# Two local-attention blocks and a gated sum in one phase

## What is computed

```python
for d in range(2):                        # two local blocks
    half = shift(x[:, C//2:], by=1)       # upper channels come from the token before
    q, k, v = split(concat(x[:, :C//2], half) @ wqkv[d])      # 8 heads of 64
    q = l2norm(q) * q_scale[d]; k = l2norm(k) * k_scale[d]
    q, k = rotate(q, k)                   # rotary angles with a scale by position
    a = softmax(q @ k.T + window_mask)    # 64-token windows, each sees itself and the one before
    x = x + (a @ v) @ wo[d]
    y = layernorm(concat(x[:, :C//2], shift(x[:, C//2:], by=1))) * ln_g[d] + ln_b[d]
    u, g = split(y @ w1[d] + b1[d])       # 341 hidden channels each
    x = x + (u * gelu(g)) @ w2[d] + b2[d]
out = x_row + silu(x) * s                 # s: output of the state-space part before it
```

## Time and profile before

| | us |
|---|---|
| median of 3 runs (4225.66 to 4240.99) | 4240.4 |
| the profiled execution | 4256.1 |
| its span, first to last instruction | 4253.9 |
| PE busy in the span | 3659.6 (86%) |
| DVE, ACT, POOL busy | 2656.3, 2155.1, 861.8 |
| mean granted clock of TensorE | 0.919 of 2.4 GHz |

### The profile page before, as it was taken

One profiled execution on the slowest core, in us unless ns is written; L12 is line 12 of the kernel. 1 busy time (PEld: TensorE's weight loads), 2 busy tenths in 40 slices (PEclk: granted clock), 3 DMA queues, 4 the chain that ended last, 5 costly groups with the idle time before them and its releaser, 6 DMA issues. The chain is left out here.

```text
span 4253.9 us, 74287 instructions
## 1 busy us (share of the span) xinstructions
PE 3659.6 (86%) x27416; PEld 2097.3 (49%) x27416; DVE 2656.3 (62%) x5977; ACT 2155.1 (51%) x4957; POOL 861.8 (20%) x1067
## 2 busy tenths in 40 slices
PE   5988878888989996899899899988878887887887
PEld 3655654444545543333333333445555665555555
DVE  5667646565555654776766767736655665665665
ACT  3555554554555453565555655754554554444454
POOL 1111000000010002122232132124212331431421
PEclk8999988988999898899999999989998998999999
DMA  3222301111101102111011111002120230321112
GB/s 107 62 48 45 77 20 47 36 24 31 36 17 43 29 13 91 28 32 38 17 43 32 23 37 33 15 38 62 37 71 23 61 80 8 79 61 27 53 42 54
DMA packets 146011, 183.15 MB, mean 43 GB/s; under 512 B 29972, under 2 KB 99796, under 8 KB 142324
## 3 DMA queue, kind: packets, MB, share of 16 engines
q1 hardware_dynamic: 139748, 170.93, 16.0%
q10 hardware_dynamic: 5904, 7.48, 0.7%
HBM read 91.69 MB, written 34.08 MB: 30 GB/s over the span
## 5 line engine op out<-in xcount | busy, mean ns | idle before, releaser
L1266 ACT ACTIVATE prob<-ps_st 128x512 f32<-128x512 f32 (+3 forms) x2432 | 1120.6, 511 | 1127.9 <-PE ps_st L1208 586.4
L1299 DVE TENSOR_REDUCE mhalf<-mx 128x1 f32<-128x512 f32 (+3 forms) x2064 | 1265.7, 652 | 658.4 <-PE mx L1240 324.4
L1237 PE MATMUL mx<-ks,qs 72*128 72x512 bf16 (+3 forms) x2304 | 793.2, 373 | 130.2 <-DVE g_tok L1874 52.5
L1205 PE MATMUL ps_st<-qs,ks 75*128 75x512 bf16 (+3 forms) x2432 | 780.5, 355 | 66.3 <-ACT prob L1266 44.5
L1188 PE MATMUL ps_o<-prob,vst 128*32 128x512 f32 (+3 forms) x5376 | 580.0, 514 | 0.1
L1237 PEld LDWEIGHTS mx<-ks,qs 72*128 72x128 bf16 x2304 | 232.4, 103 | 558.3 <-DVE mhalf L1299 192.7
L1205 PEld LDWEIGHTS ps_st<-qs,ks 75*128 75x128 bf16 x2432 | 243.1, 101 | 327.7 <-ACT prob L1266 172.1
L1349 POOL COPY vst<-v_tok 128x256 f32<-128x256 f32 x48 | 19.9, 418 | 1218.4 <-PE ps_o L1188 1217.2
L3202 ACT ACTIVATE o<-ps,nm,lrq 128x128 f32<-128x128 f32 x512 | 227.0, 462 | 43.9 <-DVE nm L3317 43.7
L1188 PEld LDWEIGHTS ps_o<-prob,vst 128*32 128x32 f32 x5376 | 114.5, 111 | 178.9 <-ACT prob L1266 78.8
L2278 POOL TENSOR_SCALAR ffn_small<-bcs,table 80x128 f32<-80x128 f32 x256 | 148.9, 603 | 122.9 <-PE mx L2406 115.6
(11 more groups left out here) (476 smaller groups left out, 6394.2 us busy)
## 6 DMA issues: line engine op xcount, KB each, us to landing
qs<-q_scr SPq DMA_DIRECT2D x279, 96.0 KB
ks<-k_scr SPq DMA_DIRECT2D x135, 192.0 KB
lkt<-o SPq DMA_DIRECT2D x256, 64.0 KB, 2.0
lve<-lv SPq DMA_DIRECT2D x24, 512.0 KB, 4.5
lqt<-o SPq DMA_DIRECT2D x160, 64.0 KB, 2.0
tabs<-local_tables SPq DMA_DIRECT2D x4, 2048.0 KB, 8.0
k_scr<-part SPq DMA_DIRECT2D x30, 256.0 KB, 3.1
lqt<-o ACTq DMA_DIRECT2D x96, 64.0 KB, 2.1
```

Of the source, the lines that this page charges most:

```text
L1205: last = nc.tensor.matmul(ps_st[:, u % 3, 0:q1 - q0], ks[g % 2][0:KR, h, kt * P:(kt + 1) * P], qs[g % 2][0:KR, hf, h, q0 - hf * HALF:q1 - ...
L1237: last = nc.tensor.matmul(bank[:, j * w:(j + 1) * w], qs[g % 2][0:R, hf, h0 + j, (t - 4 * hf) * P:(t - 4 * hf + 1) * P], ks[g % 2][0:R, h0 ...
L1266: nc.scalar.activation(prob[:, b % PROBS, h, 0:q1 - q0], ps_st[:, u % 3, 0:q1 - q0], ACT.Exp, scale=scale).then_inc(S["exped"], 1)
L1299: nc.vector.tensor_reduce(mhalf[:, hf, h0:h0 + heads, t - 4 * hf, part], bank[:, 0:heads * (k1 - k0)].rearrange("p (n w) -> p n w", n=head ...
```

## The change

`local_block` becomes a class `LocalBlock` with one program for each engine, and `local_blocks` runs both blocks and the gated sum in one phase, with semaphores of its own for each block and memory that both share. What is altered within:

- Second block on the first half: PE transposes the new rows of the first four tiles and does query/key product 0 after the last `into(5)` and before `out_of(1)` of the first block. DVE adds the new rows of the first half before the last gated value, and copies the upper channels. The transposes of the second half come after product 1.
- Buffers: the exponentials go into `net.g_tok`, the channel copies of the outputs (`och`) into `o[:, 0]`, the hidden values into `lqt`. The first exponential waits for POOL's sums and no DMA, the first `channels` for the DMA out of `o[:, 0]`. In the second block each DMA of a query piece also waits for the first block's `out_of(1)`.
- Order in the loop: on PE `weigh` of the odd unit comes in the next tile, after its first `turn`; on DVE the normalisation comes between the two copies. Six `keep_clock` products stand ahead of the loop.
- Root: for the second half of the hidden layer's normalisation POOL takes the reciprocal root (`pow` and two Newton steps) in place of ACT's square root and DVE's reciprocal. POOL adds the bias of tiles 0 to 2 after its sixth copy, that of tiles 3 to 7 after the root.
- Gated sum: Silu and the two DVE operations for each half follow the new rows of that half.

```diff
-                    local_block(net, 0)
...
-                    local_block(net, 1, ahead)
-                    gate_update(net, net.xn_tok, dst=by_tile(out[b]))
+                    local_blocks(net, ahead, by_tile(out[b]))
...
+    def queries_or_keys(pe, n):
+        m, g, i = pairs[n]
+        if n == 0 or i != pairs[n - 1][2]:
+            pe.wait_ge(S["ch_lo"], i + 1)
+            pe.wait_ge(S["ch_hi"], i + 1)
+        if before is not None and n < 2:
+            pe.wait_ge(before.S["gated"], 5 + n)
...
+    def begin_products(pe):
+        turn_rows(pe, 0)
+        if before is None:
+            turn_rows(pe, 1)
+            pe.wait_ge(S["x_first"], 1)
+        queries_or_keys(pe, 0)
...
+        for n in range(NT):
+            if n >= 2:
+                pe.wait_ge(S["v"], n - 1)
+                keep_clock(net, pv[:, n % 2, :], 5)
+                pe.wait_ge(S["prod"], 4 * (n - 1))
+                pe.wait_ge(S["sq"], 2 * (n - 1))
+            if n >= 1:
+                queries_or_keys(pe, n)
+            if n == 1:
+                if before is not None:
+                    turn_rows(pe, 1)
+                pe.wait_ge(S["ch_lo"], 2)
+                pe.wait_ge(S["ch_hi"], 2)
...
+        pe.wait_ge(S["v"], NT)
+        keep_clock(net, pv[:, 0, :], 6)
+        for t in range(NT):
+            turn(2 * t)
+            if t >= 1:
+                weigh(2 * t - 1)
+            turn(2 * t + 1)
+            if t + 2 < NT:
+                scores(t + 2)
+            if t >= 1:
+                turn_out(t - 1)
+            weigh(2 * t)
+            if t >= 2:
+                project(t - 2)
+        weigh(2 * NT - 1)
+        turn_out(NT - 1)
...
+        into(3)
+        into(4)
+        out_of(0)
+        into(5)
+        if between is not None:
+            between(pe)
+        out_of(1)
...
+            act.wait_ge(S["max"], u + 1)
+            if u == 0:
+                act.wait_ge(S["rot"], 2 * NT - 2)
...
+                if n == s == 1 and before is not None:
+                    upper_channels(dve, 1)
+                dve.wait_ge(S["sq"], 2 * n + s + 1)
...
+            if n == 0 and before is not None:
+                before.new_rows(dve, 1)
...
+        for t in range(NT):
+            if t + 1 < NT:
+                maxima(2 * t + 2)
+            if t >= 3:
+                residual(t - 3)
+            copies(2 * t)
+            if t >= 1:
+                normalise(t - 1)
+            if t + 1 < NT:
+                maxima(2 * t + 3)
+            copies(2 * t + 1)
...
+            if u == 5:
+                dve.wait_ge(S["biased"], 2)
+                new_rows(dve, 0)
+                if between is not None:
+                    between(dve)
...
+        v, r = std[:, 4:8], rstd[:, 4:8]
+        pool.wait_ge(S["spread"], 2)
+        nc.gpsimd.tensor_tensor(r, v, net.K("half").broadcast_to([P, 4]), ALU.pow).then_inc(S["root"], 1)
+        for k in (1, 5):
+            pool.wait_ge(S["root"], k)
+            nc.gpsimd.tensor_tensor(sq_r[:, :], r, r, ALU.mult).then_inc(S["root"], 1)
+            pool.wait_ge(S["root"], k + 1)
+            nc.gpsimd.tensor_tensor(sq_r[:, :], sq_r[:, :], v, ALU.mult).then_inc(S["root"], 1)
+            pool.wait_ge(S["root"], k + 2)
+            nc.gpsimd.tensor_scalar(sq_r[:, :], sq_r[:, :], -0.5, 1.5, ALU.mult, ALU.add).then_inc(S["root"], 1)
+            pool.wait_ge(S["root"], k + 3)
+            nc.gpsimd.tensor_tensor(r, r, sq_r[:, :], ALU.mult).then_inc(S["root"], 1)
+        pool.wait_ge(S["low"], NT)
+        pool.wait_ge(S["shifted"], 2)
+        bias(1)
```

More of the change, by code:

```diff
@@ L2836, in _, with __init__, local_programs @@
                         last.then_inc(S["mm"], 1)
-def local_block(net, d, ahead=()):
+class LocalBlock:
+    names = ["x_turned", "ch_lo", "ch_hi", "qkmm", "vmm", "sq", "v", "sums", "kstd", "qstd", "prod", "rot", "clamp", "kinv", "k_spread", "k_unit",
+             "placed0", "placed1", "placed2", "placed3", "small", "both", "s", "raw", "max", "exped", "tp", "copied", "o", "inv", "norm", "turned",
+             "ch", "mm", "sum", "low", "first", "sent", "shifted", "high", "stat", "var", "spread", "std", "rstd", "unit", "unit_t", "in_ch", "hid",
+             "gelu", "gated", "biased", "outp", "new", "root"]
+    own = [["x_first", "edge"], ["silu", "product", "summed"]]
+    def __init__(self, net, d, S, memory, before=None, ahead=(), out_row=None):
+        self.net, self.d, self.S = net, d, {n: S[f"{n}{d}"] for n in self.names + self.own[d]}
+        programs = local_programs(net, d, self.S, memory, before, ahead, out_row)
+        self.sync, self.tensor, self.scalar, self.vector, self.gpsimd, self.begin_products, self.begin_values, self.new_rows = programs
+def local_programs(net, d, S, memory, before, ahead, out_row):
     nc, W = net.nc, net.W
@@ new lines, in local_programs, with finished, place @@
+    ch = net.xn_ch
+    low, high = slice(0, C // 2), slice(C // 2, C)
+    placed = [S[f"placed{k}"] for k in range(4)]
+    scale = [W(f"l3_qs{d}"), W(f"l3_ks{d}")]
+    ksum = NT * H
+    def finished(queue, n, s):
+        if pairs[n][0] == 1:
+            queue.wait_ge(S["k_unit"], 2 * (n // 2) + s + 1)
+        else:
+            queue.wait_ge(S["rot"], 2 * n + s + 1)
+    def place(queue, n, s, b):
+        m, g, i = pairs[n]
+        e, j = divmod(b, 2)
+        if before is not None and m == 0:
+            queue.wait_ge(before.S["outp"], 2)
+        queue.dma_start((qt, kt)[m][D * e + 32 * s:D * e + 32 * s + 32, 2 * g + j, i * HALF:(i + 1) * HALF],
+                        o[32 * b:32 * b + 32, n % 4, s, :]).then_inc(placed[n % 4], 16)
@@ new lines, in local_programs, with turn_rows @@
+    hidden = [(c, j) for c in range(2) for j in range(3)]
+    act_g = o[:, 3, :, :].rearrange("p s (t c) -> p (s t) c", c=C)
+    def turn_rows(pe, i):
+        if before is not None:
+            pe.wait_ge(before.S["in_ch"], i + 1)
+            pe.wait_ge(before.S["new"], i + 1)
+        for j in range(4):
+            last = nc.tensor.transpose(pv[:, i, j * P:(j + 1) * P], net.xn_tok[:, 4 * i + j, :], net.ident)
+        last.then_inc(S["x_turned"], 1)
+    def queries_or_keys(pe, n):
+        m, g, i = pairs[n]
+        if n == 0 or i != pairs[n - 1][2]:
[3 more added lines that the diff above has]
+            pe.wait_ge(before.S["gated"], 5 + n)
+        for s in range(2):
+            c0 = m * IN + (2 * g + s) * P
+            last = nc.tensor.matmul(pab[:, (n + d) % 2, s, :], W(f"l3_wqkv{d}")[:, c0:c0 + P], ch[:, i * HALF:(i + 1) * HALF],
+                                    start=True, stop=True)
+        last.then_inc(S["qkmm"], 1)
```

1010 lines of the change are left out of this document (486 added, 524 removed).

## The result

The changed kernel took 4289.7 us (median of 4 runs, 4283.2 to 4309.1), the kernel before beside it 4240.7: ratio 1.0129, 95% interval 1.0095 to 1.0163. Slower, as forecast, but by 49 us where the sum gave 25. The profiled execution took 4309.1 us (span 4307.3), 53 us more than that of before.

The account below looks back on a forecast made before the run. PE, the busiest engine, was taken to bound the kernel; terms summing to +25 us on the profiled 4256.1 gave 4281, scaled to the median 4265 us. The forecast's own range was 4250 to 4277, with rivals 4214 to 4290.

Parts of the forecast that it names:

- the loop: Attention loop, scores(5) to scores(7): odd half's weighing leaves the circle, PE's own work sets the pace; -5 us.
- its end: Scores(7) to the last output transposes: nothing covers DVE's last normalisation, so they come 1.1 us later per block; +9 us.
- scores(4) earlier: Before scores(4): exponentials skip the DMA wait, gain cut by SP's pieces; -19 us, and +2 for query-piece waits.
- Gated sum: End of each row: table load and first half lie beside the last output product; -2.95 us in four rows, -12.
- Hand-over: First to second block: early start removes PE idle time in one place, adds it in another; -1 us.
- Clock behind the root: Behind PE's wait of 3.4 us for the gated value: lower clock costs 2.5 us in eight blocks, +20.
- Root: Second normalisation: POOL's root takes 2.3 us and its bias slows DVE's unit rows; +1.8 us in eight blocks, +14.
- the rival with the slow root: Rival at POOL's root: pow is dear, the root takes 3.5 us; +10, 4275 us; chance 0.15.
- Clock behind scores(4): PE idle 2.4 to 3.6 us before scores(4), then 6.83 us at 1.2 GHz in six of eight blocks; +19 us.
- the clock holds: Rival: TensorE stays at 2.4 GHz through the gaps before scores(4) and at the root; -39, 4226 us; chance 0.12.
- DVE is not held: Rival: unit rows run before or beside POOL's bias, root costs 0.5 us, clock stays; 4234 us; chance 0.13.

Follow-up runs that it names:

- exp_waits_pieces: Changed kernel with the first exponentials again waiting for the placed pieces, still written to the other buffer: 4278.4 us, ratio 1.0076 to the kernel before.
- root_alone: Kernel before the change with only the second layer-norm root moved to POOL (power and eight refining steps): 4271.3 us, ratio 1.0067.
- fill_handover: Changed kernel with 10 idle products on TensorE in the second block's start, before the second value product: 4281.1 us, ratio 1.0093 to the kernel before.
- no_early_start: Changed kernel with the second block begun only behind the first one's out_of(1) and second new rows, still one phase: 4279.8 us, ratio 1.0082 to the kernel before.
- bias_after_units: Changed kernel with POOL's bias of rows 3 to 7 held until VectorE has written all eight units: 4278.0 us, ratio 1.0065 to the kernel before.

## Why the prediction was right and wrong

Right: the direction, and what carries it. The root on POOL with the bias holding DVE, and the clock behind PE's pause, were together the largest positive part of the sum (+34), and taking the root back removes the whole loss. Of the other terms the loop (-6.0 for -5) and its end (+8.0 for +9) came as worked out. scores(4) earlier (-18.4 for -19 and +2) is right in size and partly by luck: the term put all of it down to the early exponentials, but with these taken back (exp_waits_pieces) the stage is still 8.8 us shorter than before (418.2 for 427.0), and root_alone, whose code there is that of before, has 420.0.

Wrong: the sum fell 28 us short of the 53 between the profiles (24 of the 49 between the medians). The steps that failed are two above all, the gated sum's gain followed no further than its store, and no clock given to the pause in the hand-over; a third, the root's own length, was sized too small. In the order of size in the profiles:

- *Gated sum*, -12: each row's store did go out 2.9 us earlier, but the step ended there. It did not follow the gain into the next phase, where another pause of PE and a longer low clock took it back (+1.3 in place of -9 for three rows), nor see that 117 semaphores are cleared behind the last store (+4.6 once). Missed by 15 us.
- *Hand-over*, -1: the sum held the clock against pauses in other places and itself worked out a new pause at the second value product (upper channels at +13.0), but gave that one no clock. It was 2.58 to 2.93 us, and the clock fell in three of four. Missed by 9 us here, by 6 to 7 on the mean of eight kernels; fill_handover shows the cause. The 1.1 us that the phase without a meeting gives, which no_early_start brings out, were not seen.
- *Clock behind the root*: +28.6 for +20. The low clock was taken as 6.8 us; it was 10.2 in six blocks and 6.8 in two, 3.6 us lost on the mean for 2.5. This is a draw more than an error: over the seven kernels with the same code there it was 22 us, close to the forecast's 20.
- *Root*: +19.8 for +14; the stage is the same 61.8 us in all seven kernels that have root and bias as the kernel after. Nine operations in 3.25 us and not 2.3: the power 1.02 us, each further one 0.20 and 0.08 to the next. It is near the rival with the slow root (3.5 us), which was given 0.15.
- *Clock behind scores(4)*: +13.7 (10.7 and the 3.0 that the loop's order gave back in this step) for +19, in the other direction. It fell in all eight blocks, for 6.8 us in six and 3.4 in two, but 2.0 to 3.9 us of the 6.8 lay in the pause itself, where they cost nothing.

The rival "the clock holds" fell in all sixteen places (eight at the root, eight at scores(4)); "DVE is not held" fell by the 2.08 us. The statement that no pause over 2.5 us kept the clock, true of the trace before, fell too: one of 2.58 us at 3064.66 did, and 13 of 32 in the hand-overs of eight kernels, four of these after 2.93 us. The Trainium skill (TensorE: Matmul & The Clock Gate, section "HAM oscillation — how this bites in real kernels") tells of a kernel whose waits for data between batches of matmuls bring the half rate back every time; the traces agree at the root for pauses of 2.98 us and more (eight of eight in each kernel without idle products there), and not for those of 2.58 to 2.93 us in the hand-over.

## What to carry to other kernels

Price every new pause of TensorE twice, for its length and for the clock behind it, in the phases that follow as well. Here the second was as large as the first (22 to 28 us and 23 at the root), and it varies by itself, so take it from several profiles. A gain of 3 us a row disappeared in a pause 35 us further on. Where a pause can't be removed, idle products about as long as the pause were nearly free here, but only while something else set its end; once that was gone they were on the path. A chain of tiny dependent operations belongs on the engine that does it in the fewest instructions: counted from the start of the spread, one square root and a reciprocal took 0.9 us, nine POOL operations 3.6.

## What the runs showed of the hardware

- POOL on 128x4: a power 1.02 us, a product or a multiply-and-add 0.20, with 0.08 from one to the next that depends on it.
- In front of into(2) a pause of TensorE of 2.98 to 3.02 us brought the 1.2 GHz level each time (eight of eight, bias_after_units), one of 3.95 to 4.2 us too (56 of 56, seven kernels); in the hand-over one of 2.58 to 2.93 us did in 19 of 32. The low stretch at the same pause of 3.95 us was 3.4, 6.8 or 10.2 us in different rows and kernels, costing 1.3 to 1.7, 2.2 to 2.9, or 3.8 to 4.2 us in the same work (into(2) to out_of(0), 6.79 without). So equal code differs from row to row, and the stage summed over eight blocks from profile to profile (70.8 to 82.9 us).
- DVE's 128x128 tensor-scalar, four in 1.12 us alone, took 2.08 beside a POOL addition of 1.32 us.
- Between the last store's issue and the end of the span lay 8.3 us with 117 semaphores to clear and 4.6 with 60 of them.
